# Graph layer with rotations: the pairs' loop inverts, moves and applies one group in the same pass

## The reference, cut to what matters

```
xn = layernorm(x)                                   # x: 6250 x 256
M = I                                               # 256 x 256
for (i, j, theta) in edges:                         # 100,000, in order
    M[i], M[j] = cos*M[i] - sin*M[j], sin*M[i] + cos*M[j]
gnn = xn @ M.T
query, key, value = xn Wq + bq, xn Wk + bk, xn Wv + bv
lam = softmax(key, over rows).T @ value             # 256 x 256
bn  = batchnorm(lam);  mix = query @ bn
x = x + gnn + mix
x = x + ffn(layernorm(x))                           # 8 experts, the best 2 of each row
```

## Time and profile before

| | |
|---|---|
| median of 3 runs (lowest to highest) | 734.21 us (733.88 to 734.66) |
| the profiled execution: time, span | 737.21 us, 735.3 us |
| mean granted clock | 0.928 |
| PE busy in the span | 644.6 us, 88% |
| DVE, ACT, POOL busy | 472.9, 449.9, 388.6 us |
| chain that ended last: PE, DVE, "issue" | 67%, 9%, 7% |
| pass of the loop, first product of the inversion to the last copy | 205.71 to 222.53 us |
| its tail, to the first transpose of turned0 | 222.53 to 236.69 us |

### The profile page before, as it was taken

The page is one execution under the profiler, slowest core; times in us unless marked ns, Lnnn a source line. Parts: engine busy times, 40 slices in busy tenths (PEclk is TensorE's granted clock), DMA queues, the critical chain, the costliest instruction groups (busy, mean ns, idle before and its releaser), DMA issues.

```text
span 735.3 us, 18134 instructions
## 1 busy us (share of the span) xinstructions
PE 644.6 (88%) x4079; PEld 551.3 (75%) x4080; DVE 472.9 (64%) x1877; ACT 449.9 (61%) x1235; POOL 388.6 (53%) x532
## 2 busy tenths in 40 slices
PE   5789899754798998059999999899989999999996
PEld 4457577532687776048998999899979999999996
DVE  5797666699865799333544444344457777777775
ACT  6777666487234699336665666566656666666663
POOL 6104777145434177715776777323246656666554
PEclk8899999955599999569999999999999999999999
DMA  8830112246400477622443334222223333333332
GB/s 241 229 88 12 22 31 23 52 142 203 142 27 2 125 225 218 199 71 95 140 138 123 120 119 131 70 69 62 69 79 103 101 98 103 106 102 96 107 97 69
DMA packets 60873, 78.10 MB, mean 106 GB/s; under 512 B 15868, under 2 KB 49488, under 8 KB 60570
## 3 DMA queue, kind: packets, MB, share of 16 engines
q1 hardware_dynamic: 45703, 42.94, 21.0%
q0 software_dynamic: 14544, 34.11, 13.9%
q10 hardware_dynamic: 576, 0.54, 0.3%
HBM read 47.53 MB, written 31.53 MB: 108 GB/s over the span
## 4 chain that ended last, share of the span: by engine, by line
PE 67%; DVE 9%; issue 7%; DMA 5%; POOL 4%; ACT 4%; SPq 2%; DVEq 0%; POOLq 0%; ACTq 0%
PE banks L2716 22%; PE banks L2726 20%; PE banks L2324 5%; PE banks L2668 5%; PE banks L2303 4%; POOL send_d L903 3%; PE banks L2707 3%; DMA R<-in_edge_weight_dram 1%; DMA R<-send_d 1%; DMA out_dram<-R,dest_now 1%; PE banks L2314 1%; DVE R L1760 1%; PE banks L2429 1%; PE banks L2294 1%; PE banks L2419 1%
## 5 line engine op out<-in xcount | busy, mean ns | idle before, releaser
L2716 PE MATMUL banks<-R 128*128 128x128 f32 x1696 | 210.4, 278 | 3.6 <-ACT R L1288 3.5
L2716 PEld LDWEIGHTS banks<-R 128*128 128x128 f32 x1696 | 201.1, 194 | 4.6 <-ACT R L1288 4.5
L2726 PE MATMUL banks<-R 128*128 x848 | 200.4, 379 | 0.0
L1301 ACT ACTIVATE R<-banks,b1c 128x128 f32<-128x128 f32 x424 | 142.9, 363 | 54.2 <-PE banks L2716 53.8
L2726 PEld LDWEIGHTS banks<-R 128*128 128x128 f32 x848 | 153.1, 191 | 16.4
L1288 ACT ACTIVATE R<-banks,bet_c,gam_c 128x128 f32<-128x128 f32 x212 | 85.4, 453 | 114.8 <-PE banks L2707 112.3
L2211 DVE COPY R<-R 128x1024 f32 x106 | 74.3, 701 | 77.6 <-PE banks L2716 59.8
L903 POOL DMA_INDIRECT send_d<-R,slot_all x98 | 98.5, 1005 | 45.7 <-issue 40.6
L916 POOL DMA_INDIRECT first_d<-R,dest_now x54 | 61.0, 1130 | 94.4 <-DVE R L2216 79.4
L925 POOL DMA_INDIRECT R<-first_d,get_now x52 | 53.7, 1033 | 48.9 <-DVE get_now L2193 46.8
L916 POOL DMA_INDIRECT out_dram<-R,dest_now x52 | 63.3, 1217 | 29.8 <-issue 26.5
(11 more groups left out here) (553 smaller groups left out, 957.0 us busy)
## 6 DMA issues: line engine op xcount, KB each, us to landing
R<-send_d SPq DMA_DIRECT2D x106, 131.0 KB
R<-in_L_ffn_W_dram SPq DMA_DIRECT2D x16, 512.0 KB, 4.5
R<-in_x_dram SPq DMA_DIRECT2D x14, 512.0 KB, 4.6
R<-in_x_dram SPq DMA_DIRECT2D x5, 1024.0 KB, 12.4
send_d<-zrow SPq DMA_DIRECT2D x14, 131.0 KB, 5.2
send_d<-R,slot_all POOLq DMA_INDIRECT x98
erec_d<-R SPq DMA_DIRECT2D x1, 1400.0 KB
R<-in_L_ffn_b_dram SPq DMA_DIRECT2D x1, 1024.0 KB, 5.6
```

The costliest lines, as they stand in the source:

```text
L1301: last = nc.scalar.activation(hT[b][:, c, :], bank[2 + 2 * b + c // 2][:, (c % 2) * P:(c % 2 + 1) * P], ACT.Gelu, bias=b1c[:, bass.ds(e, 1 ...
L2716: last = mm(bank[2 + 2 * b + c // 2][:, (c % 2) * P:(c % 2 + 1) * P], w1c[b][:, kb, c * P:(c + 1) * P], xmT[b][:, kb * P:(kb + 1) * P], st ...
L2726: last = mm(bank[6 + b][:, 0:D], hT[b][:, c, :], w2s[:, bass.ds(e, 1), c, :].rearrange("p a h -> p (a h)"), start=(c == 0), stop=(c == H / ...
```

## The change

Pass k now inverts, moves and applies its own group k; nothing of an empty group is applied, and the tail behind the loop has no transform and no applying any more. Semaphore counts shift accordingly (a new one, writes_seen, tells DVE that count_writes is done). The six constants ahead of added_row go; router_sums stands in their place, and added_logits and DVE's copies out of the added row come ahead of the loop, in bank 6. Three memsets move to earlier places on DVE. The split of addrow moves ahead of POOL's loop. base_T and its copy by ACT go: DVE multiplies Mrot by flush in place, adds flush to its last column, and adds PSUM bank 1 to it. Three constants stand in front of the transposes where ten stood.

```diff
@@ POOL
             gather_steps(2)
-            pool.wait_ge(S["ngroups"], 1)
-            n = pool.value_load(n_groups_i[0:1, 0:1], min_val=1, max_val=4 * NE)
-            with loop(pool, 0, n) as k:
-                fields(k + 2)
-                gather_steps(k + 3)
-            pool.wait_ge(S["recs_in"], n * (16 * G) + 3 * 16 * G)
+            pool.wait_ge(S["recs_in"], 3 * 16 * G)
             settle(pool)
             pool.wait_ge(S["addrow_ok"], 1)
             pl = chain(pool, S["addparts_ok"])
...
             pool.sem_inc(S["parts_made"], 1)
+            pool.wait_ge(S["ngroups"], 1)
+            n = pool.value_load(n_groups_i[0:1, 0:1], min_val=1, max_val=4 * NE)
+            with loop(pool, 0, n) as k:
+                fields(k + 2)
+                gather_steps(k + 3)
+            pool.wait_ge(S["recs_in"], n * (16 * G) + 3 * 16 * G)
+            settle(pool)
@@ ACT
             def scaled(k, which, gs):
-                    act.wait_ge(S["GT_psum"], k * 2 + 2)
+                    act.wait_ge(S["M_done"], k * G + 1)
...
             def last_writes(k):
-                act.wait_ge(S["M_psum"], k * (2 * G) + 2 * G)
+                act.wait_ge(S["M_done"], k * G + 1)
...
             with loop(act, 0, n) as k:
-                moved_GT(k)
                 left_of_L(k)
                 better(k, 0)
-                apply_v(k, 0)
                 scaled(k, 0, (0, 1))
                 better(k, 1)
-                apply_v(k, 1)
                 scaled(k, 0, HALVES[1])
                 better(k, 2)
-                apply_v(k, 2)
                 scaled(k, 1, (0, 1))
                 better(k, 3)
                 scaled(k, 1, HALVES[1])
                 better(k, 4)
                 inverse_so_far(k)
                 last_writes(k)
                 better(k, 5)
+                moved_GT(k)
+                apply_v(k, 0)
                 pair_angles(k + 2)
-            moved_GT(n)
-            apply_v(n, 0)
-            apply_v(n, 1)
-            act.wait_ge(S["pe"], BASE)
-            nc.scalar.activation(base_T, bank[1]..., ACT.Copy).then_inc(S["comb_moved"], 1)
-            apply_v(n, 2)
+                apply_v(k, 1)
+                apply_v(k, 2)
             table_of(ACT.Sqrt)
@@ DVE
             def kept(k):
-                dve.wait_ge(S["M_done"], k * G + (G + 1))
+                dve.wait_ge(S["writes_seen"], k + 1)
+                dve.wait_ge(S["M_done"], k * G + 1)
...
             dve.wait_ge(S["empty_group"], 1)
+            dve.wait_ge(S["pe"], ROW_ADDED)
+            nc.vector.tensor_copy(add_c[:, :], bank[6][:, AT_ADD:AT_ADD + KB])
+            TT(brB[:, :], bank[6][:, AT_SUMS + NX:AT_SUMS + 2 * NX], brB[:, :], ALU.add)
+            nc.vector.tensor_copy(addrow[:, 0:D], bank[6][:, 0:D])
+            for kb in range(KB):
+                last = STT(comb[:, kb, D + NX:AVG], bank[6][:, AT_SUMS:AT_SUMS + NX], -1.0 / D, wrg[:, kb, :], ALU.mult, ALU.add)
+            last.then_inc(S["setup_own"], 1)
             first_guess(0)
+            dve.wait_ge(S["setup_own"], 1)
+            own(nc.vector.tensor_reduce(addrow[:, AVG:AVG + 1], addrow[:, 0:D], AX_X, ALU.add))
+            TS(addrow[:, AVG:AVG + 1], addrow[:, AVG:AVG + 1], 1.0 / D, None, ALU.mult)
             find_last(0)
+            dve.wait_ge(S["pe"], LOGIT_ADDED)
+            nc.vector.tensor_copy(addrow[:, D:D + NX], bank[6][:, AT_LOGITS:AT_LOGITS + NX]).then_inc(S["addrow_ok"], 1)
...
                 other_rows(k)
+                factor(k, 1)
                 find_hits(k1, (0, 1))
-                factor(k, 1)
-                apply_m(k, 0)
+                factor(k, 2)
                 find_hits(k1, HALVES[1])
-                factor(k, 2)
+                factor(k, 3)
                 find_latest(k1)
-                apply_m(k, 1)
-                factor(k, 3)
+                factor(k, 4)
+                rows_read(k)
+                factor(k, 5)
+                kept(k)
                 mark_latest(k1)
-                apply_m(k, 2)
-                factor(k, 4)
                 own_reads(k1)
                 other_part(k1)
                 build_L(k1)
-                factor(k, 5)
-                rows_read(k)
+                apply_m(k, 0)
+                first_guess(k1)
                 find_last(k1)
-                kept(k)
-                first_guess(k1)
+                apply_m(k, 1)
+                apply_m(k, 2)
...
+            dve.wait_ge(S["M_done"], n * G + 1)
             for kb in range(KB):
+                last = TS(Mrot[:, kb, :], Mrot[:, kb, :], flush[:, 0, kb:kb + 1], None, ALU.mult)
+            own(last)
+            own(TT(Mrot[:, :, D - 1], Mrot[:, :, D - 1], flush[:, 1, :], ALU.add))
             dve.wait_ge(S["recs_in"], n * (16 * G) + 3 * 16 * G)
             dve.wait_ge(S["flds_ready"], n + 2)
             dve.wait_ge(S["Y_ready"], n + 1)
-            for kb in range(KB):
-                last = STT(turned0[:, kb, :], Mrot[:, kb, :], flush[:, 0, kb:kb + 1], base_T[:, kb, :], ALU.mult, ALU.add)
-            last.then_inc(S["combT_ok"], 1)
+            dve.wait_ge(S["pe"], BASE)
+            TT(turned0, bank[1]..., Mrot[:, :, :], ALU.add).then_inc(S["combT_ok"], 1)
@@ PE
             pe.wait_ge(S["ngroups"], 1)
-            for _ in range(6):
-                mm(bank[6][:, 0:P], ident[:, :], ident[:, :], start=True, stop=True)
+            router_sums()
             added_row()
             turn_L(0)
             count_later(0)
+            added_logits()
             with loop(pe, 0, n) as k:
-                transform(k)
                 residual(k, 0)
                 spread_targets(k + 1)
                 better(k, 0)
-                apply_v(k, 0)
                 residual(k, 1)
-                apply_m(k, 0)
                 better(k, 1)
...
                 residual(k, 5)
                 count_writes(k)
+                better(k, 5)
+                transform(k)
+                apply_v(k, 0)
+                apply_m(k, 0)
                 count_later(k + 1)
                 turn_L(k + 1)
-                better(k, 5)
-            transform(n)
-            apply_v(n, 0)
-            added_logits()
-            apply_m(n, 0)
+                apply_v(k, 1)
+                apply_m(k, 1)
+                apply_v(k, 2)
+                apply_m(k, 2)
             base_rows(0)
-            apply_v(n, 1)
-            apply_m(n, 1)
             base_rows(1).then_inc(S["pe"], 1)
-            apply_v(n, 2)
-            apply_m(n, 2)
-            for _ in range(10):
-                mm(TB[:, 0:P], ident[:, :], ident[:, :], start=True, stop=True)
+            for _ in range(3):
+                mm(bank[0][:, 0:P], ident[:, :], ident[:, :], start=True, stop=True)
             pe.wait_ge(S["combT_ok"], 1)
```

More of the change, by code:

```diff
@@ L189, in gnn_layer @@
         col0b = chunk(D, dt=BF16)
-        PT, base_T = [chunk(KB, D) for _ in range(2)]
+        PT = chunk(KB, D)
         lam = R1[:, at_both - KB * D:at_both].rearrange("p (k d) -> p k d", k=KB)
@@ L1815, in build_composites @@
                 dve.wait_ge(S["pe"], VALUES)
+                nc.vector.memset(addrow[:, D + NX:DC], 0.0)
                 for kb in range(KB):
@@ L1881, in _ @@
             last.then_inc(S["wrg_ok"], 1)
+            nc.vector.memset(comb[:, :, AVG:DC], 0.0)
+            nc.vector.memset(addparts[:, :], 0.0)
             dve.wait_ge(S["xn_ready"], NG12 + 1)
@@ L2448, in count_writes @@
                     for kb in range(KB):
-                        mm(misc[:, g * KB + kb:g * KB + kb + 1], Rt[:, g, kb * P:(kb + 1) * P], last16[:, g:g + 1],
-                           start=True, stop=True)
+                        last = mm(misc[:, g * KB + kb:g * KB + kb + 1], Rt[:, g, kb * P:(kb + 1) * P], last16[:, g:g + 1],
+                                  start=True, stop=True)
+                last.then_inc(S["writes_seen"], 1)
             def transform(k):
                 pe.wait_ge(S["M_done"], k * G + 1)
-                pe.wait_ge(S["B_ready"], k + 1)
+                pe.wait_ge(S["B_ready"], k + 2)
                 for g in range(G):
                     if g % 2 == 0:
-                        pe.wait_ge(S["Y_done"], k * NEWT + (g // 2 + 1))
+                        pe.wait_ge(S["Y_done"], k * NEWT + (NEWT + g // 2 + 1))
                     for kb in range(KB):
@@ L2556, in added_logits @@
                 for a in range(KB):
-                    last = mm(misc[:, AT_LOGITS:AT_LOGITS + NX], add_c[:, a:a + 1].broadcast_to([P, P]), comb[:, a, D + NX:AVG],
+                    last = mm(bank[6][:, AT_LOGITS:AT_LOGITS + NX], add_c[:, a:a + 1].broadcast_to([P, P]), comb[:, a, D + NX:AVG],
                               start=(a == 0), stop=(a == KB - 1))
```

43 lines of the change are left out of this document (10 added, 33 removed).

## The result

**738.78 us, median of 20 executions, against 734.09 for the kernel before beside it (20): ratio 1.0045, 95% interval 1.0025 to 1.0064. Slower by 0.45%**, where 730.5, faster, was forecast. (Two executions of the changed kernel, at 800 and 1341 us, were disturbed; they and the slowest of the others, 743.30, are left out of the ratio but not of the median.) That is rival C's side, and more than its 736.1. The profiled execution took 739.56 us, its span is 737.7 us and its mean granted clock 0.915 (before: 737.21, 735.3, 0.928).

What follows compares the result with a forecast made beforehand. It took the chain of waits, in the inversion's levels their latency, as the bound. Start 0.6, pass 3.7, applying 0.2, less 0.9 for the clock, gave 3.7 us with rounding: from 734.21 to 730.5 us, range 728.2 to 733.5.

Steps and rivals of the forecast that it cites:

- rival C: Clock stays at 1.2 GHz through the whole inversion, decided by the fourth level; 1.9 us lost, 736.1, slower; chance 0.10.
- The step that failed: Inversion's first levels: pass starts at 1.2 GHz, clock rises within the second level; costs 0.9 us, between 0 and 4.2.
- The start: Ahead of the loop: router sums replace constants and the empty group's transform; first product at 205.1, 0.6 us earlier.
- The pass: Pairs' loop: without foreign matmuls (another group's, on PE), the inverse is there at 13.1 instead of 16.8, 3.7 us gained.
- The applying: After the inverse, moved into the pass: turned0 14.0 us after it, now 14.16 to the first transpose; 0.2 gained.
- The gather: End of the applying: DVE waits for the next group's unused records, ending the stretch 1.05 us later than base_rows would.
- POOL's split: Splitting addrow (4.7 us) moves ahead of the loop's fields and costs nothing, covered by POOL's 7.19 us wait for angles.
- the chain that bounds a level: Inversion level: product, W on DVE, product, copy on ACT, each waiting for the one before; latency bounds it, 2.1 us.
- D: The change does not shorten the pass, as the empty group's matmuls only filled waits; 0.8 us gained, 733.4; chance 0.10.
- the one-to-one carry to the end: After the tail: the sums release all that follows, so a gain at turned0's first transpose carries fully to the end.
- Rival B: Clock falls in the last levels; transform and part of the first applying run at half speed, 2.3 us, 732.8; chance 0.15.
- A: Ahead of the loop, the clock rises by 203 as now; no level is slow, 5.4 us gained, 728.8; chance 0.22.

Runs made afterwards that it cites:

- g0: The changed kernel run once more, unaltered: 738.61 us, ratio 1.0029.
- e2: Changed kernel with constant matmuls behind the products of the inversion's levels, none ahead of the loop: 734.19 us, ratio 0.9987.
- h1: Changed kernel with constants filling set-up waits, around added row and logits, and in levels; PE reads n earlier, DVE waits for records later: 731.8 us, ratio 0.9957.
- e3: Kernel before without its six constant matmuls ahead of the added row: 734.78 us, ratio 0.9997.
- h4: h3 with POOL reading n ahead of its split of addrow, and the split waiting for DVE's one-hot rows: 730.78 us, ratio 0.9935.
- h3: h1 with DVE reading n ahead of its wait for the added row: 734.01 us, ratio 0.9983.
- h2: h1 with POOL's split of addrow put back behind POOL's loop: 735.79 us, ratio 0.9996.
- f3: f2 with DVE's wait for the next group's records moved behind comb's columns: 734.42 us, ratio 0.9976.
- f2: Changed kernel with nine constant matmuls in the set-up's waits and constants behind the levels' products: 734.92 us, ratio 0.9985.
- i1: Kernel before with ten constants ahead of HISTORY, router sums and six constants ahead of SCALES, its own six kept: 735.44 us, ratio 0.9999.
- f1: Changed kernel with nine constant matmuls in set-up waits, six ahead of HISTORY and three ahead of SCALES: 737.1 us, ratio 1.0027.

## Why the prediction was wrong, and where it was right

**The step that failed** is "I take it that the pass starts at 1.2 GHz and the clock rises within the second level, since at the low level a level's twelve records (12 x 0.24 at full width) leave PE hardly a pause in it", with 0.10 for C. By their mean clock, 11 of 18 executions, and 7 of 12 in g0, are of the kind of the profiled one, in which the clock does not rise before the transform. In that one PE was busy 18.33 of 19.21 us at 0.50, so few pauses, the reason given, did not bring the rise. C had "decides by the fourth level" and priced the inversion at 3.3 us more than the forecast; between the two profiles of the changed kernel it is 3.88 (19.21 against 15.33) for the inversion and 0.81 (15.57 against 14.76) for the rest, where C had 2.3.

The clock is not the whole miss. The median, 738.78, lies 8.3 us above the forecast. The high group, in whose profile (g0) the clock did rise as forecast, lies 3.0 us above it (733.46), and the low group another 6.8 (740.28). So the terms of the sum were too good as well, and C's total, which stands on them, came out too low for the same reason.

The page that the prediction named, the Trainium skill, "TensorE: Matmul & The Clock Gate", Part 1 (activity releases the throttle), agrees with e2 and h1, in which more matmuls raise or hold the clock. The profiled execution of the changed kernel does not bear it out: at 95% busy by the profile the clock stayed at 0.50. The prediction applied the rule to the constants in front only; e3 shows that the old order does without these.

**The terms, at the high clock.** g0's stretch, 38.12, stands 3.1 us above the 35.0 that the sum gave (38.64 less 3.6):
- *The start*: 8.03 us from SCALES instead of 7.2 (205.1 less 197.89). PE's pause in front of the loop, 0.43 as "issue" in the chain, was not counted; it is gone there in h1, which reads n earlier and has 0.50 of it behind SCALES. Row and logits took 0.2 each more at the low clock.
- *The pass*: 15.33 instead of 14.0 (13.1 and 0.9 for the clock). Levels three to five took 2.34, 2.27 and 2.13, close to the 2.1. The first two took 6.54 where 2.1, 2.5 and 0.9 make 5.5. The clock is not all of it: at 1.00 throughout they take 6.86 in h1 and 5.05 in h4. Between these two stand DVE's reading of n in front of the first W (h3: the first level goes from 3.23 to 2.44) and POOL's split, moved to the same time, which makes DVE's copies and rows longer (h2: the second level from 3.63 to 2.60). The prediction counted neither.
- *The applying*: 14.76 instead of 14.0. The gather did end the stretch. Without that wait it is 13.94 (220.35 to 234.29 in f3). Its cost was 0.2 in f2 to 0.8 in g0, where 1.05 was forecast. A round is 3.31 us (230.04 to 233.35), not 3.0.

**POOL's split** was costed at nothing on POOL, with L837's wait as its cover; that held (8.62 us idle there, 1.98 in g0, 7.19 before). What it does to DVE was left out. The Trainium skill, "SBUF — State Buffer", section "Who interferes with whom", says that a copy, cast or tensor_scalar of DVE in a two-port mode and a GpSimd instruction exclude each other; by that rule the move had a price. The trace agrees: L1652, a copy, takes 0.53 us beside the split in h1 and 0.18 without it in h2.

**What was right**: the chain that bounds a level and its 2.1 us; that the pass shortens by the foreign matmuls (D refuted by e2, h1 and i1); the one-to-one carry to the end (the first transpose is 2.3 us later than before, 238.85 against 236.53, the span 2.4). From h4's first product to the transposes there are 28.11 us, where "about 28" stood, but that is partly luck: h4 has the clock at 1.00 throughout and no wait for the gather in front of turned0, and the prediction's sum without its 0.9 for the clock and its 1.05 for the gather would be about 26. Rival B occurred in f1, with 1.44 us (16.20 against 14.76) where it had 2.3. No profile of the changed kernel without added matmuls shows A.

**Still open**: what decides in a given execution whether the clock rises in the second level or not before the transform; two traces with the same instructions differ in it.

## What to carry to other kernels

Before you take out work that only fills TensorE's waits, look in the trace at what then keeps the clock up: here 33 records fewer in the pass, none of them on the path by its result, went with a loss of 0.45%. With others in their place, and with n read earlier, the split later and the wait for the records later, there was a gain of 0.65%. Sort the executions by their granted clock before you believe a median; here two separate groups pointed to the clock, and only within one group could the order of the work be judged. And a small block moved to where its own engine idles has to be looked up on the engines that then run beside it: POOL's split cost POOL nothing and DVE 1.0 us on the chain.

## What the runs showed of the hardware beyond that

- In one execution a granted clock of 0.50 stays through 27 us (196.04 to 223.28) in which PE is busy 95% of the time by the profile. In another execution of the same kernel (g0) it rises 12 us behind SCALES.
- Reading n and starting a loop costs each engine time in front of it. On PE it is 0.43 us. On DVE the idle time from the last copy to the first W is 1.45 us in h1 and 0.50 in h3, which reads n earlier. On POOL there are 3.98 us "issue" between split and fields in h1, and still 3.25 with n read earlier (h4).
